# A recurrent cell with four sets of weights: gate-ordered weight columns, the output gate turned by itself, 256 columns ahead of the choice

## The reference, cut to what matters

```
i, f, g, o = split(gates, 4)
c_new = sigmoid(f) * c + sigmoid(i) * tanh(g)
h_new = sigmoid(o) * tanh(c_new)

def step((h, c), x_t):
    logits = concat([h, c, x_t]) @ W_sel.T + b_sel         # 4 logits
    s = argmax(logits)
    gates = x_t @ W_ih[s].T + h @ W_hh[s].T + b_ih[s] + b_hh[s]   # 4 x 512
    return lstm_activate(gates, c)
```

## Time and profile before

| | |
|---|---|
| median of three timed runs | 7232.47 us |
| profiled execution, first to last instruction | 7418.4 us |
| TensorE busy in it (matmul) | 6208.6 us, 84% |
| TensorE weight loads | 4093.6 us, 55% |
| VectorE, ScalarE, GpSimd busy | 2599.8, 1699.7, 894.9 us |

### The profile page before, as it was taken

How to read it: one execution, slowest core, us unless ns; L and a number is a source line. 1 busy time by engine, 2 the same in 40 slices (tenths; PEclk the granted TensorE clock), 3 DMA queues, 4 the chain that set the end, 5 groups by cost and what they waited for, 6 DMA issues and landing times. The chain is left out here.

```text
span 7418.4 us, 494613 instructions
## 1 busy us (share of the span) xinstructions
PE 6208.6 (84%) x211307; PEld 4093.6 (55%) x211307; DVE 2599.8 (35%) x12046; ACT 1699.7 (23%) x8390; POOL 894.9 (12%) x2042
## 2 busy tenths in 40 slices
PE   6857999999999999999779997999889987888731
PEld 5524555555555555555467775777667765666520
DVE  5334444444444421111233332333233332222257
ACT  0122333333333333333101111111111111111111
POOL 0011111111111288000000000000000000000000
PEclk9978999999999999999889999999999999999965
DMA  1011111111111111000042221222112211111100
GB/s 45 0 49 32 29 30 29 31 29 30 30 29 31 33 42 41 0 0 0 14 129 40 44 41 15 39 40 42 24 29 43 40 32 7 7 7 7 20 13 7
DMA packets 814823, 213.43 MB, mean 29 GB/s; under 512 B 706441, under 2 KB 772653, under 8 KB 814724
## 3 DMA queue, kind: packets, MB, share of 16 engines
q1 hardware_dynamic: 765700, 152.75, 10.7%
q0 software_dynamic: 47872, 54.13, 2.7%
q10 hardware_dynamic: 1152, 5.15, 0.2%
HBM read 183.50 MB, written 28.16 MB: 29 GB/s over the span
## 5 line engine op out<-in xcount | busy, mean ns | idle before, releaser
L1756 PE MATMUL ps_rows<-whh,h_pair 128*4 128x320 f16 x34944 | 1321.0, 302 | 112.8 <-issue 29.9
L1074 PE MATMUL ode_busy<-ode_busy_x,ode_busy_w 128*32 128x384 f16 (+4 forms) x18816 | 1261.9, 328 | 25.9 <-issue 16.4
L1756 PEld LDWEIGHTS ps_rows<-whh,h_pair 128*4 128x4 f16 x34944 | 744.9, 84 | 542.7 <-DVE h_pair L1613 155.1
L1068 PEld LDWEIGHTS ode_psa<-ode_a,ode_w2t 128*32 128x32 f32 x19968 | 433.7, 110 | 749.3 <-ACT ode_a L1181 587.7
L1625 DVE COPY gate_rows<-ps_rows_last 128x192 f32<-128x192 f32 x624 | 223.0, 357 | 1570.7 <-PE ps_rows_last L1756 1570.7
L1191 DVE SCALAR_TENSOR_TENSOR ode_part<-ode_b 128x1 f32<-128x1 f32 x624 | 110.7, 177 | 1795.1 <-ACT ode_b L1183 1793.7
L1677 ACT COPY gate_rows<-ps_rows 128x320 f32<-128x320 f32 x624 | 265.8, 426 | 1726.0 <-PE ps_rows L1756 1726.0
L1183 ACT ACTIVATE ode_b<-ode_psa 128x1 f32<-128x1 f32 x2496 | 427.5, 171 | 1005.0 <-PE ode_psa L1068 1005.0
L1068 PE MATMUL ode_psa<-ode_a,ode_w2t 128*32 128x1 f32 x19968 | 611.6, 181 | 26.0 <-ACT ode_a L1175 13.4
L1085 PE MATMUL ode_pso<-whh 125*32 125x170 f32 (+3 forms) x9600 | 602.6, 319 | 31.2 <-issue 31.2
L1756 PE MATMUL ps_rows_last<-whh,h_pair 128*4 128x192 f16 x19968 | 527.0, 248 | 7.0 <-issue 7.0
(11 more groups left out here) (499 smaller groups left out, 9795.2 us busy)
## 6 DMA issues: line engine op xcount, KB each, us to landing
late_w<-in_wih_t SPq DMA_DIRECT2D x386, 128.0 KB, 2.1
xg_buf<-xg_scratch SPq DMA_DIRECT2D x1248, 16.0 KB, 2.0
split_raw<-in_whh_t SPq DMA_DIRECT2D x64, 256.0 KB, 2.6
ig_w<-in_wih_t SPq DMA_DIRECT2D x8, 2048.0 KB, 10.9
xg_scratch<-late_out SPq DMA_DIRECT2D x24, 624.0 KB, 3.2
whh<-h_scratch SPq DMA_DIRECT2D x105, 62.5 KB, 2.2
xg_scratch<-ig_out ACTq DMA_DIRECT2D x8, 628.0 KB, 8.6
h_scratch<-mlp_h SPq DMA_DIRECT2D x40, 125.0 KB, 2.3
```

Source lines behind the costliest of these rows:

```text
L1068: m = nc.tensor.matmul(ps[32 * j:32 * j + 32, 0:1], w[:, 32 * j:32 * j + 32], col, start=start, stop=stop, skip_group_check=True)
L1074: nc.tensor.matmul(ps_busy[32 * j:32 * j + 32, 0:cols], busy_w[:, 32 * j:32 * j + 32], busy_x[:, 0:cols], start=True, stop=True, skip_grou ...
L1756: m = nc.tensor.matmul(out[32 * j:32 * j + 4, :], hpair[:, c, 2 - 2 * part:6 - 2 * part], whh[:, at + lo:at + hi], start=(part == 0 and c ...
```

## The change

The columns of `W_hh` are ordered by gate (input, cell, forget, output: `BLOCK_GATE`) and no longer by blocks of units, so a block of 128 columns is one gate. Ahead of the choice, 256 columns are multiplied (input and cell gate) and no longer 320. The rest is done in two pieces of 128 columns, the forget gate into `ps_rows_forget` and the output gate, last, into `ps_rows_out`; VectorE copies each piece by itself. The input's part of the output gate has matmuls and a bank (`ps_out_gate`) of its own. TensorE turns the input and cell gates, then the forget gate, and signals `gates`; then one late matmul; then it waits for the copy of the output gate, turns it, signals `out_gate`, and does the other late matmul. ScalarE takes tanh of 12 gate columns, then, after `out_gate`, of the 4 others. VectorE makes c first and the output gate after it; `wgated` now starts from the tanh of the output gate. Two sets share a bank of `ps_rows`. The layouts on the host, a scale and a few memsets follow.

```diff
-    FIRST = 5 * 64
+    FIRST = 2 * 128
+    IFG = 3 * KC
...
-                    nc.vector.scalar_tensor_tensor(parts[:], act[:, 0:8], 1.0, act[:, 12:20], ALU.add, ALU.mult).then_inc(S["fi"], 1)
-                    nc.vector.tensor_scalar(ok[:], act[:, 8:12], 1.0, 1024.0, ALU.add, ALU.mult).then_inc(S["o"], 1)
+                    nc.vector.scalar_tensor_tensor(parts[:], act[:, 0:2 * KC], 1.0, act[:, 2 * KC:4 * KC], ALU.add, ALU.mult).then_inc(S["fi"], 1)
                     v.wait_ge(S["fi"], k + 1)
                     nc.vector.scalar_tensor_tensor(ccur, parts[:, KC:2 * KC], 0.5, parts[:, 0:KC], ALU.mult, ALU.add).then_inc(S["c_ready"], 1)
+                    v.wait_ge(S["out_acted"], k + 1)
+                    nc.vector.tensor_scalar(ok[:], out_tanh[:], 1.0, 1024.0, ALU.add, ALU.mult).then_inc(S["o"], 1)
+                    nc.vector.scalar_tensor_tensor(wgated[:], out_tanh[:].unsqueeze(2).broadcast_to([128, KC, PAIRS]), 1.0, wsel[:, 0:KC, :], ALU.add, ALU.mult).then_inc(S["w_ready"], 1)
+
                     v.wait_ge(S["o"], k + 1)
-                    nc.vector.tensor_tensor(wgated[:], wsel[:, 0:KC, :], ok[:].unsqueeze(2).broadcast_to([128, KC, PAIRS]), ALU.mult).then_inc(S["w_ready"], 1)
...
-                    v.wait_ge(S["rows_last"], k)
-                    nc.vector.tensor_copy(gsb[:, FIRST:D], psb[:, 0:D - FIRST]).then_inc(S["evac_v"], 1)
+                    v.wait_ge(S["rows_forget"], k)
+                    nc.vector.tensor_copy(gsb[:, 256:384], psf[:, 0:128]).then_inc(S["evac_f"], 1)
+                    v.wait_ge(S["rows_out"], k)
+                    nc.vector.tensor_copy(gsb[:, 384:512], pso[:, 0:128]).then_inc(S["evac_o"], 1)
...
-                    nc.scalar.activation(act[:, 0:16], psc[:, 0:16], ACT.Tanh).then_inc(S["acted"], 1)
+                    nc.scalar.activation(act[:, 0:IFG], psc[:, 0:IFG], ACT.Tanh).then_inc(S["acted"], 1)
+                    a.wait_ge(S["out_gate"], k + 1)
+                    nc.scalar.activation(out_tanh[:], psq[:, 0:KC], ACT.Tanh).then_inc(S["out_acted"], 1)
...
                             for part in range(2):
                                 for c in range(KC):
-                                    m = products(e, part, c, psb[:, 0:D - FIRST], FIRST, D)
-                            m.then_inc(S["rows_last"], 1)
+                                    m = products(e, part, c, psf[:, 0:128], 256, 384, (part, c) == (0, 0))
+                            m.then_inc(S["rows_forget"], 1)
+                            for part in range(2):
+                                for c in range(KC):
+                                    m = products(e, part, c, pso[:, 0:128], 384, 512, (part, c) == (0, 0))
+                            m.then_inc(S["rows_out"], 1)
                             for j in range(4):
-                                m = nc.tensor.matmul(psc[32 * j:32 * j + 32, 0:16], ident[:, 32 * j:32 * j + 32], xgb[:, q, :, e * 8:(e + 1) * 8], start=True, stop=False, skip_group_check=True)
+                                nc.tensor.matmul(psc[32 * j:32 * j + 32, 0:IFG], ident[:, 32 * j:32 * j + 32], xgb[:, q, e * 16:e * 16 + IFG], start=True, stop=False, skip_group_check=True)
+                            for j in range(4):
+                                m = nc.tensor.matmul(psq[32 * j:32 * j + 32, 0:KC], ident[:, 32 * j:32 * j + 32], xgb[:, q, e * 16 + IFG:(e + 1) * 16], start=True, stop=False, skip_group_check=True)
                             m.then_inc(S["xg_used"], 1)
...
                         pe.wait_ge(S["evac_a"], k)
-                        turn(0)
-                        turn(1)
-                        turn(2, (0, 1))
-                        pe.wait_ge(S["evac_v"], k)
-                        turn(2, (2, 3))
-                        turn(3).then_inc(S["gates"], 1)
-
-                        if block is not None:
-
-                            for c in range(q * PER, (q + 1) * PER):
-                                m = nc.tensor.matmul(ps_late[:, 0:BLOCK], late_w[:, c * 128:(c + 1) * 128], xt[:, c, ds(block * BLOCK + EARLY, BLOCK)], start=(c == 0), stop=(c == KC - 1))
-                            m.then_inc(S["late_used"], 1)
+                        turn(psc[:, 0:KC], 0, False)
+                        turn(psc[:, 2 * KC:3 * KC], 1, False)
+                        pe.wait_ge(S["evac_f"], k)
+                        turn(psc[:, KC:2 * KC], 2, True).then_inc(S["gates"], 1)
+                        late(0)
+                        pe.wait_ge(S["evac_o"], k)
+                        turn(psq[:, 0:KC], 3, True).then_inc(S["out_gate"], 1)
+                        late(1)
```

More of the change, by code:

```diff
@@ L1461, in _ @@
                 v.wait_ge(S["bias"], 1)
-                nc.vector.memset(scale[:].rearrange("p (s q) -> p s q", s=CELLS)[:, :, 3 * KC:], 1.0).then_inc(S["bias"], 1)
+                nc.vector.memset(scale[:].rearrange("p (s q) -> p s q", s=CELLS)[:, :, 2 * KC:3 * KC], 1.0).then_inc(S["bias"], 1)
                 v.wait_ge(S["bias_in"], 32)
@@ L1515, in sb @@
             return ctx.enter_context(nc.sbuf_tensor(name, shape, dt))
-        xgb = sb("xg_buf", [128, UN, 2, CELLS * 8])
+        xgb = sb("xg_buf", [128, UN, CELLS * 16])
         xg0 = sb("xg_first", [128, 16])
@@ L1538, in stage_lstm @@
         S = {k: new_semaphore(nc, "lstm_" + k) for k in (
-            "xg0_in", "init", "c_ready", "o", "w_ready", "h_made", "hp_ready", "logits", "best", "rows_first", "rows_last", "evac_a", "evac_v",
-            "gates", "acted", "fi", "tanh_c", "kept", "seen_v", "seen_a", "seen_g", "seen_pe", "xg_used", "late_used", "late_moved", "late_stored")}
+            "xg0_in", "init", "c_ready", "o", "w_ready", "h_made", "hp_ready", "logits", "best", "rows_first", "rows_forget", "rows_out", "evac_a", "evac_f", "evac_o",
+            "gates", "out_gate", "acted", "out_acted", "fi", "tanh_c", "kept", "seen_v", "seen_a", "seen_g", "seen_pe", "xg_used", "late_used", "late_moved", "late_stored")}
         with nc.Block() as block:
@@ L1676, in move @@
                             a.wait_ge(S["rows_first"], k)
-                            nc.scalar.copy(gsb[:, 0:FIRST], psg[:, e * BANK:e * BANK + FIRST]).then_inc(S["evac_a"], 1)
+                            nc.scalar.copy(gsb[:, 0:FIRST], psg[:, e * FIRST:(e + 1) * FIRST]).then_inc(S["evac_a"], 1)
                         with a.If(s < 1 << 16):
@@ L1733, in _ @@
                 pe.wait_ge(S["kept"], 1)
-                nc.tensor.matmul(psc[:, 0:16], ident[:], xg0[:], start=True, stop=True).then_inc(S["gates"], 1)
+                nc.tensor.matmul(psc[:, 0:IFG], ident[:], xg0[:, 0:IFG], start=True, stop=True).then_inc(S["gates"], 1)
+                nc.tensor.matmul(psq[:, 0:KC], ident[:], xg0[:, IFG:16], start=True, stop=True).then_inc(S["out_gate"], 1)
                 def turn_of_two(i, block):
@@ L1750, in turn_of_two, with products @@
                         m.then_inc(S["logits"], 1)
-                        def products(e, part, c, out, lo, hi):
+                        def products(e, part, c, out, lo, hi, start):
                             for j in range(4):
@@ L1756, in products @@
                                 m = nc.tensor.matmul(out[32 * j:32 * j + 4, :], hpair[:, c, 2 - 2 * part:6 - 2 * part], whh[:, at + lo:at + hi],
-                                                     start=(part == 0 and c == 0), stop=(part == 1 and c == KC - 1), skip_group_check=True)
+                                                     start=start, stop=(part == 1 and c == KC - 1), skip_group_check=True)
                             return m
                         def first(e, part, c):
-                            return products(e, part, c, psg[:, e * BANK:e * BANK + FIRST], 0, FIRST)
+                            return products(e, part, c, psg[:, e * FIRST:(e + 1) * FIRST], 0, FIRST, part == 0 and c == 0 and e % 2 == 0)
                         pe.wait_ge(S["hp_ready"], k)
@@ L1795, in turn_of_two @@
                                 recurrent(0)
-                        def turn(c, quarters=range(4)):
-                            for j in quarters:
-                                m = nc.tensor.matmul(psc[32 * j:32 * j + 32, c:16:4], gsb[:, c * 128 + 32 * j:c * 128 + 32 * j + 32], gsel[:], start=False, stop=(c == KC - 1), skip_group_check=True)
-                            return m
-                        pe.wait_ge(S["evac_a"], k)
-                        turn(0)
-                        turn(1)
@@ L1806, in turn_of_two, with turn @@
-                        turn(2, (0, 1))
-                        pe.wait_ge(S["evac_v"], k)
-                        turn(2, (2, 3))
-                        turn(3).then_inc(S["gates"], 1)
-                        if block is not None:
-                            for c in range(q * PER, (q + 1) * PER):
-                                m = nc.tensor.matmul(ps_late[:, 0:BLOCK], late_w[:, c * 128:(c + 1) * 128], xt[:, c, ds(block * BLOCK + EARLY, BLOCK)], start=(c == 0), stop=(c == KC - 1))
```

(20 more changed lines are left out.)

37 lines of the change are left out of this document (20 added, 17 removed).

## The result

The changed kernel takes 13,587.01 us (median of four runs, 13,576.43 to 13,601.45), the kernel before in the same job 7232.35 (7225.18 to 7232.89): a ratio of 1.879, 95% interval 1.877 to 1.882. The forecast was 14,386 us.

What follows compares the result with a forecast made beforehand. A closed chain, TensorE its longest link, bounds the kernel at 5.036 us a step. After, 312 turns x 33 = 10,296 us replace 3142.8: 7418.4 + 7153 = 14,572, less 186 is 14,386 us; range 13,600 to 15,800, from 11,600 with rival 2.

Steps and rivals of the forecast that it cites:

- The step that decides: TensorE's program size: a two-step loop body needs 10 pages, the store keeps 8, so every turn reloads them.
- rival 1: The program fits because 10 to 12 pages are kept; about 7200 us, chance 0.14.
- The price: Loading TensorE's program: 3.46 us a page, 10 pages a turn of two steps, taken as 33 us a turn.
- rival 2: Pages not run cost nothing, only some 7 loads a turn (24.2 to 28 us); 12,200 us, chance 0.2.
- Rival 3: Pages have fixed places, so only those sharing one collide; +8 us a turn, 9700 us, chance 0.04.
- The small steps: Changes within a step's chain (products, choice, copy, turn, late matmuls), summed without the program's size to -82 us.
- Fours of 128 columns: TensorE's products: four matmuls of 128 columns cost 0.056 us, by a line through the 320- and 192-column pitches.
- The wait for the choice: After the branch, TensorE waits 0.21 us for the chosen weights; last product +0.09 us.
- An ordinary step: A cell step without late matmuls: 4.57 us, -0.34 us (bounds -0.45 and +0.1).
- one with late matmuls: A cell step with late matmuls gains nothing: 4.91 us (bounds -0.3 and +0.2).
- the late matmul's part: One late matmul call ahead of the output gate's turn on TensorE delays what follows by about +0.33 us.

Runs made afterwards that it cites:

- pad_same: The kernel before with 53 never-run matmuls behind an untaken branch in each copy of sets 0, 2 and 3; 13,479.06 us, ratio 1.864.
- short_copies: The changed kernel with the copies of sets 2 and 3 cut to the last four matmuls of each piece; 7139.84 us, ratio 0.987 to the kernel before.
- pad_n21: The kernel before with 21 never-run matmuls behind an untaken branch in each copy of sets 0, 2 and 3; 8075.62 us, ratio 1.117.
- gate384: The changed kernel with input, cell and forget gates as one 384-column piece, late matmuls after the output gate's turn; 7128.26 us, ratio 0.986 to the kernel before.
- pad_edge: The kernel before with 22 never-run matmuls behind an untaken branch in each copy of sets 0, 2 and 3; 7261.29 us, ratio 1.0047.
- pad_n30: The kernel before with 30 never-run matmuls behind an untaken branch in each copy of sets 0, 2 and 3; 10,927.83 us, ratio 1.512.

## Why the prediction was right

**The step that decides** held: the body touches more pages than are kept, and each turn loads them all. Both halves were shown apart (pad_same has the size without the chain, short_copies the chain without the size), and the store's 8 pages are exact: rival 1 needed 10 to 12, and 9 already don't fit. That number was a bet all the same: the rows left 8 to 12 open, and a power of two decided.

**The price** is the term that was mis-sized. 33 us a turn was chosen between 31 and 34.6; it is 30.48. 312 x 2.52 = 786 us, and 14,386 - 786 = 13,600: this one term is the whole miss, and it puts the time 13 us under the lower end of the forecast's own range, inside the range that takes in rival 2. The 3.46 us of a page that is awaited came near (3.5 in the fit without a constant); a page that is only loaded ahead costs 1.9 and not 3.46, and loop three, in 78 of the 312 turns, loads 9 pages and not 10. That last is a step that failed: a page's successor was to be asked for when the page is entered, and 54 instructions in loop three's last page don't call for it. The lower end that the prediction worked out, 7 x 3.46 = 24.2 and the idle loads beside it, about 31, was the better reading.

**Rival 2** (pages that aren't run cost nothing) falls with the same table: with 7 pages run, each more that is only loaded ahead adds some 2 us. It was right in part, since such a page costs less than one that is run. **Rival 3** (fixed places) falls with the 9 or 10 loads of nearly every turn.

**The small steps**, hidden beside the loads in the changed kernel, are seen in short_copies. Fours of 128 columns: (0.62 - 0.22) / 7 = 0.057 us apart, 0.056 expected. The wait for the choice: 0.31 for 0.21. An ordinary step 4.615 for 4.57, one with late matmuls 4.966 for 4.91, the late matmul's part of it 0.35 for 0.33. Over all steps that is -0.285 x 240 + 0.066 x 384 = -43 us where -82 was forecast, mostly because the late steps lose a little where nothing was expected.

## What to carry to other kernels

Count the instructions of a loop's body on its engine, copies that are jumped over included, and lay it on the pages that the trace shows, before the shapes and waits are weighed: here one page too many cost some 18 us a turn, in a chain that takes within 0.3 us a step of the old one where its program fits. Near the border, the place of the body counts as well as its size: with 12 instructions fewer a body, pad_n21's loop two starts 11 instructions before a page border and not on it, and its turn takes three times as long. A piece that is split to shorten a chain multiplies by the number of copies of the code around it; the same order with wider pieces (gate384) fits, and is 1.4% faster than before.

## What the runs showed that was not expected

- A smaller program can be slower: pad_n21, 12 instructions fewer a body than pad_edge, takes 8075.62 us and not 7261.29.
- A page loaded ahead counts among the 8 as forecast, but costs only about 1.9 us a turn.
- A loop at the border can alternate: pad_n30's loop two loads 1 or 2 pages in one turn and 8 or 7 in the next.
